# Cross-attention reciprocals spread over the partitions by a DRAM store and a repeating load, and the engines' orders written anew

## What is computed

```python
x = _layernorm(x + _L0_attn_ref(x, ...))      # theta = .5 + .2*sigmoid(qk) + .15*tanh(qk) + .1*relu(qk); softmax
x = _layernorm(x + _L0_xattn_ref(x, ctx, ctx, ...))   # softmax(q k / 4) v in chunks of 64, 16 heads
x = _layernorm(x + _L0_ffn_ref(x, ...))       # 4 of 32 experts per token, and a shared expert
```

## Time and profile before

| what | us |
|---|---|
| median of 3 runs (lowest to highest) | 883.02 (879.79 to 887.2) |
| the profiled execution | 873.37 |
| its span, first to last instruction | 871.2 |
| PE busy in the span | 801.1 (92%) |
| DVE busy | 546.1 (63%) |
| ACT busy | 461.5 (53%) |
| POOL busy | 408.3 (47%) |

### The profile page before, as it was taken

How to read it: one execution, slowest core, us unless ns; L and a number is a source line. 1 busy time by engine, 2 the same in 40 slices (tenths; PEclk the granted TensorE clock), 3 DMA queues, 4 the chain that set the end, 5 groups by cost and what they waited for, 6 DMA issues and landing times.

```text
span 871.2 us, 23658 instructions
## 1 busy us (share of the span) xinstructions
PE 801.1 (92%) x7881; PEld 658.8 (76%) x7881; DVE 546.1 (63%) x2115; ACT 461.5 (53%) x1150; POOL 408.3 (47%) x501
## 2 busy tenths in 40 slices
PE   7778999999999999999999555899999999999885
PEld 6567788888888888888887444688888888887332
DVE  2244577887788787887788852355555555554366
ACT  1455566655665666655665111466666666665133
POOL 0200235464455546464545662455656555556123
PEclk9999999999999999999999875999999999999999
DMA  6472223243324322342331124855555555552996
GB/s 222 125 174 79 80 69 103 100 136 93 121 76 142 106 103 82 133 124 94 104 127 58 67 86 134 301 163 166 165 162 159 169 165 158 161 170 91 327 401 242
DMA packets 69654, 125.06 MB, mean 144 GB/s; under 512 B 9665, under 2 KB 43329, under 8 KB 69282
## 3 DMA queue, kind: packets, MB, share of 16 engines
q1 hardware_dynamic: 51394, 81.60, 30.3%
q0 software_dynamic: 13776, 37.77, 12.1%
q10 hardware_dynamic: 4368, 4.20, 1.4%
HBM read 73.16 MB, written 50.36 MB: 142 GB/s over the span
## 4 chain that ended last, share of the span: by engine, by line
PE 78%; DMA 6%; POOL 5%; issue 4%; SPq 4%; ACT 2%; DVE 1%; ACTq 0%; POOLq 0%; DVEq 0%
PE banks L584 15%; PE banks L274 11%; PE banks L597 7%; PE banks L393 4%; SPq L623 4%; PE banks L381 3%; PE banks L354 3%; PE banks L314 3%; PE banks L335 3%; PE banks L371 3%; PE banks L326 3%; PE banks L487 3%; PE banks L518 3%; PE banks L541 3%; PE banks L529 3%
## 5 line engine op out<-in xcount | busy, mean ns | idle before, releaser
L1431 POOL DMA_INDIRECT y<-yb_tile,idcol_tile x159 | 153.0, 962 | 123.6 <-ACT yb_tile L948 121.3
L584 PE MATMUL banks<-w_expert_tile,xbT_tile 128*128 x636 | 166.4, 385 | 3.9 <-ACT xbT_tile L786 3.9
L584 PEld LDWEIGHTS banks<-w_expert_tile,xbT_tile 128*128 128x128 f32 x636 | 109.9, 193 | 13.5 <-issue 4.9
L1259 DVE COPY hbT_tile<-banks 128x128 f32<-128x128 f32 x159 | 46.4, 292 | 117.2 <-PE banks L274 117.2
L1398 POOL DMA_INDIRECT routed<-row_tile,idx_tile x64 | 63.3, 989 | 85.0 <-PE banks L410 66.5
L948 ACT ACTIVATE yb_tile<-banks,rowsb_tile 128x256 f32<-128x256 f32 x159 | 75.4, 474 | 48.8 <-PE banks L597 41.5
L597 PE MATMUL banks<-w_expert_tile,hbT_tile 128*128 x318 | 95.7, 383 | 0.0
L1366 POOL TENSOR_TENSOR rs_tile<-ve_tile,half_neg_tile 128x2 f32<-128x2 f32 x16 | 11.5, 717 | 140.6 <-DVE ve_tile L1046 140.6
L1405 POOL DMA_INDIRECT routed<-row_tile,idx_tile x64 | 65.7, 1027 | 17.7 <-issue 17.7
L942 ACT ACTIVATE gb_tile<-banks 128x128 f32<-128x128 f32 x159 | 44.2, 278 | 55.5 <-PE banks L584 55.5
L786 ACT ACTIVATE xbT_tile<-banks 128x256 f32<-128x256 f32 x159 | 59.9, 377 | 25.5 <-PE banks L274 25.2
(11 more groups left out here) (205 smaller groups left out, 1847.0 us busy)
## 6 DMA issues: line engine op xcount, KB each, us to landing
rowsb_tile<-routed SPq DMA_DIRECT2D x159, 129.0 KB, 2.2
w_expert_tile<-y SPq DMA_DIRECT2D x15, 1024.0 KB, 16.6
w_expert_tile<-w_expert SPq DMA_DIRECT2D x16, 768.0 KB, 6.3
cT_tile<-ctxT SPq DMA_DIRECT2D x16, 384.0 KB, 3.4
routed<-zrow_tile SPq DMA_DIRECT2D x1, 4128.0 KB, 22.7
xT_tile<-xT SPq DMA_DIRECT2D x16, 256.0 KB, 3.2
x_sb_tile<-x SPq DMA_DIRECT2D x16, 256.0 KB, 3.5
base<-acc_sb_tile SPq DMA_DIRECT2D x16, 256.0 KB, 3.8
```

What stands on the lines that cost most here:

```text
L584: m = e.matmul(bank[2 + u % 2][:, 0:2 * EI], xbT[u % 2][:, k * P:(k + 1) * P], w_flat[:, bass.ds(w + k * D, D)], start=k == 0, stop=k == D ...
L1259: e.tensor_copy(hbT[u % 2][:, :], bank[4 + u % 2][:, 0:EI]).then_inc(SEM["v_hbT"], 1)
L1431: e.indirect_dma_start(y, bass.IndirectOffsetOnAxis(ap=idcol[n % ROWS][:, :], axis=0), yb[n % YS][:, :], None).then_inc(SEM[f"st_y{n % YS} ...
```

## The change

- `pe_spread`, its constant and `act_num` go. `rden` (128x64) is stored to the DRAM buffer `rdd` and loaded back by two DMAs into `rsp`, each row repeated over 16 partitions. `o` reads av2's result from PSUM and `rsp` from SBUF.
- `row` and `idx` exist twice (`kM`, `vM`, `mxa` too). `pool_row` becomes `act_row`: one ACT instruction that writes all four copies.
- The PSUM banks and the order of each engine are new. Cross-attention's second half is one turn later (`scores2(t - 2)`, `x2T(t - 4)`, `shared_out(t - 5)`), so there are 22 turns.
- For space, `t12`, `prT`, `x1T` and one `kM` lie in the last 3072 columns of the expert weights (`LATE = 2` shares); those two shares are loaded in turns 17 and 18.

```diff
+        def store_den(e, i):
+            e.wait_ge(SEM["v_rden"], i + 1)
+            after(e, SEM["ld_den"], 16 * DK * i)
+            e.dma_start(rdd[i % 2].rearrange("r c q -> c r q"), rden[i % 2][:, :]).then_inc(SEM["st_den"], 16)
+        def load_den(e, i):
+            e.wait_ge(SEM["st_den"], 16 * (i + 1))
+            after(e, SEM["v_o"], i)
+            for g in range(DK):
+                e.dma_start(rsp[:, g, :], rdd[i % 2, g * 8:(g + 1) * 8].rearrange("r c (o q) -> r o (c q)", o=1)
+                            .to_broadcast([8, HD, S])).then_inc(SEM["ld_den"], 16)
...
         def vec_o(e, i, ch):
-            e.wait_ge(SEM["p_spread"], i + 1)
-            e.wait_ge(SEM["a_num"], i + 1)
-            e.tensor_tensor(f, bank[7][:, :], f, ALU.mult).then_inc(SEM["v_o"], 1)
+            e.wait_ge(SEM["p_av2"], i + 1)
+            e.wait_ge(SEM["ld_den"], 16 * DK * (i + 1))
+            e.tensor_tensor(num[:, :, :].rearrange("p a b -> p (a b)"), bank[3][:, :],
+                            rsp[:, :, :].rearrange("p a b -> p (a b)"), ALU.mult).then_inc(SEM["v_o"], 1)
...
+        def act_row(e, i):
+            e.wait_ge(SEM["a_x2"], i + 1)
+            after(e, SEM[f"st_rowa{i % 2}"], 16 * TOPK * (i // 2))
+            after(e, SEM[f"st_rowb{i % 2}"], 16 * TOPK * (i // 2))
+            e.activation(row[i % 2][:, :, :, 0:D],
+                         x2[i % 2][:, :, :].rearrange("p (k t) d -> p k t d", k=1).to_broadcast([P, TOPK, T, D]), ACT.Copy)\
+                .then_inc(SEM["a_row"], 1)
...
@@ SP
-            for t in range(nseq + 5):
+            for t in range(nseq + 6):
...
+                if live(t - 2):
+                    store_den(e, t - 2)
+                if live(t - 2):
+                    load_den(e, t - 2)
+                if 0 < t <= nseq - LATE:
                     load_rest(e, t - 1)
```

More of the change, by code:

```diff
@@ L70, in constants @@
     at, out = 0, {}
-    for name, a in zip(("ident", "before", "ones", "headmask", "denmask", "spread", "region", "upto", "blockno", "part", "nowhere"), parts):
+    for name, a in zip(("ident", "before", "ones", "headmask", "denmask", "region", "upto", "blockno", "part", "nowhere"), parts):
         out[name] = (at, a.shape[1])
@@ L158, in build @@
         den = sa("den", [P, T])
-        prT = sa("prT", [P, T, T, P])
+        prT = late(1024, 512).rearrange("p (t u q) -> p t u q", t=T, u=T)
         xc = sa("xc", [P, T, D])
@@ L167, in build @@
         x1 = sa("x1", [P, T, D])
-        x1T = sa("x1T", [P, DK, S])
+        x1T = late(2560, 512).rearrange("p (k s) -> p k s", k=DK)
         half_neg = sa("half_neg", [P, T])
         qT = sa("qT", [P, DK, S])
-        kM = sa("kM", [P, DK, S // CH, 2, CH])
-        vM = sa("vM", [P, T, NP, VW])
-        mxa = sa("mxa", [P, 4, 4])
+        kM = [sa("kM0", [P, DK, S // CH, 2, CH]),
+              late(1536, 1024).rearrange("p (k n h c) -> p k n h c", k=DK, n=S // CH, h=2)]
+        vM = [sa(f"vM{u}", [P, T, NP, VW]) for u in range(2)]
+        mxa = [sa(f"mxa{u}", [P, 4, 4]) for u in range(2)]
         mxb = [sa(f"mxb{u}", [P, 4, 4]) for u in range(2)]
@@ L189, in build @@
         acc_sb = sa("acc_sb", [P, T, D])
-        row = sa("row", [P, TOPK, T, RW])
+        rsp = sa("rsp", [P, DK, S])
+        row = [sa(f"row{u}", [P, TOPK, T, RW]) for u in range(2)]
         sc = sa("sc", [P, T, E])
@@ L208, in build @@
         slot = sa("slot", [P, T, 8])
-        idx = sa("idx", [P, T, TOPK], I32)
+        idx = [sa(f"idx{u}", [P, T, TOPK], I32) for u in range(2)]
         ctx_a.close()
@@ L1284, in _ @@
             e.memset(ev[:, :, :], -BIG)
[L1285 removed]
+            for u in range(2):
+                e.memset(vM[u][:, :, :, :], 0.0)
             ch(e.memset(macc[:, :, :], 0.0))
             e.wait_ge(SEM["g_iota"], 1)
[L1288 removed]
+            for u in range(2):
+                m = e.tensor_scalar(row[u][:, :, :, D + 1].bitcast(I32), dest_id[:, :, :], float(u * T), None, ALU.add)
+            ch(m)
             e.wait_ge(SEM["ld_const"], 16 * 5)
```

467 lines of the change are left out of this document (224 added, 243 removed).

## The result

The changed kernel takes 909.59 us (median of 4 runs, 906.94 to 919.38); the kernel before took 881.40 beside it (4 runs). The ratio is 1.033, 95% interval 1.024 to 1.043: slower, where 864.0 and a range of 855 to 880 were forecast.

The account below looks back on a forecast made before the run. PE alone was taken to set the time in mid-part. Fill 129.5, eleven turns of 27.27 and drain 69 gave 498.5 against 519.2; with 1.7 allowed, 19 less than the median 883.02: 864.0 us, range 855 to 880.

Parts of the forecast that it names:

- The step that failed: On POOL, in full turns: 2.3 us of copies go, which were off the path, so no gain or loss.
- four rivals: A and B, plus fill and drain giving nothing (872, chance 0.10) and spread's time not given back (880, chance 0.06).
- SP's queue: Next turn's xT stands behind the store, both loads and weights: 25.4 us after z against 27.27, covered by 1.9.
- A: Rival: a trip of 7.0 makes DVE's loop 27.9, some 3.5 of 19 us left, 879 us; chance 0.11.
- B: Rival: both legs at 3.8, a trip of 8.3 that sets the turn, 900 us; chance 0.09.
- the trip: Between rden and o: store, landing, two loads, landing; 5.2 us, lower bound 4.6, upper 8.3.
- DVE's rest of the loop: DVE's work besides the trip: 20.9 us, with the trip 26.1, 1.2 shorter than PE's turn.
- the spread: On PE, 1.03 us per sequence goes, so a full turn falls from 28.30 to 27.27 us if PE stays fed.
- the row copy: On ACT, one instruction of 2048 columns, about 2.1 us, with 2 us to spare before av1.
- the last stretch: From key(15) to the first row load: the same 12.5 us of scatters and landing in both kernels.
- The fill: Turns 0 to 4: xT(2) at 56, then 23, 23 and 25.5, plus 2 for the clock; turn 5 at 129.5 us.
- The drain: After the eleven full turns until key(15) is done: 21 + 21 + 25, plus 2 for the clock, 69 us.

Follow-up runs that it names:

- e1: Changed kernel with POOL's first four scatters waiting for av2 instead of scores2, so none runs beside den: 877.37 us, 0.999 of the kernel before.
- e2: Changed kernel with SP issuing the next turn's xT, x and cT loads before the store of the reciprocals: 887.63 us, 1.010 of the kernel before.
- e5: Kernel before with one group of four POOL scatters moved to wait for pTb, beside av2 and den: 916.31 us, ratio 1.038.
- e12: e3 plus four plain 129 KB stores per turn from POOL beside v and den: 882.67 us, 1.007 of the kernel before.
- e3: Changed kernel with both edits, scatters after av2 and next turn's loads before the store: 863.14 us, 0.982 of the kernel before.
- e7: e3 with the store of the reciprocals made twice, one after the other, for a longer trip: 899.94 us, 1.020 of the kernel before.
- e10: e3 plus four unused POOL additions of 128x256 per turn beside v and den: 873.41 us, 0.994 of the kernel before.
- e9: e3 with the 4128 KB zero fill cut into eight stores over turns 5 to 12: 856.24 us, 0.975 of the kernel before.

## Why the prediction was wrong

*The step that failed* is "POOL loses 2.3 us of copies, which were off the path in full turns: nothing". It asked what the edit takes off POOL, and not what the new orders put beside POOL's scatters on PE. den's 1.1 us went into the turn as a fixed price, "if PE stays fed"; in the full turns of before no scatters stand beside it, so the price held only for that neighbourhood. That it was no fixed price could be read there already: the same 32 instructions took 3.2 us in turns 1 and 2. Beside scatters den costs 2.2 us more in each turn, with a lower clock behind it in some (0.55 to 0.60 over 3.8 us). e1 (off), e2 (left on) and e5 (on in the old kernel) show it from three sides. In `after` it makes most of the difference in the eleven full turns: they took 332.1 instead of 300, of which 11 x 2.2 is 24 and the clock in four of them some 7. None of my four rivals was this one.

*Mis-sized: SP's queue.* I had xT at 25.4 after z, covered by 1.9. The loads' issue took 1.22 and not 0.9, xT's landing 6.5 and not 5.2, and den's delay came on top: rden starts at z + 18.3 instead of 16.5. Even with den at 1.1, in e1, five turns wait for xT. The forecast's sign for "A or B", a z that waits for xT, did appear in the fill, but neither A nor B held: the trip was 5.8. SP's queue made z(5) 7.8 later than forecast, and e2 takes 9.6 off there.

*Nearly right: the trip.* 5.8 us against 5.2, far from B's 8.3. The store's leg was 2.07 us, the nearest rows had 2.5 and 3.8. Two terms of mine stand on no row: the 2.0 a leg of the lower bound, beside which the store's leg was 2.07, and the 0.2 for two wake-ups, of which the first, from rden's end to the store's issue, took 0.03 (305.78 to 305.81). B's 3.8 a leg was not reached by a store alone in a full turn. With other transfers in flight the store's leg was 3.20 in e12, and 6.13 in turn 2 of e3, behind the zero fill. DVE's rest of the loop was right (20.9; e7: 20.33 + 0.55), so the cover was 0.6, and e7 and e12 show that a longer trip costs time beyond it.

*Right: the spread*, 1.03 a turn. e3's turn is 27.25 against 27.27, without any idle time on PE. *Right: the row copy*, 1.92 us on ACT, and *the last stretch*, 12.8 from key(15) to the row load.

*The fill.* xT(2) came at 55.3 (56 forecast); turns 2 to 4 took 28.4, 25.4 and 28.2 instead of 23, 23 and 25.4. z waited 2.4 us for xT at the end of turns 2 and 3, and the granted clock was low in two of the turns that such a wait stands before (0.89 in the mean of turn 2, 0.94 in turn 4), but 1.00 in turn 3; with the loads first, e2 and e3 have 1.00 in turn 4, which takes 25.97. e3 has z(5) at 127.3, close to my 129.5 but made up otherwise: z(2) at 48.4 and turn 2 of 28.7.

*The drain was too short.* From scores2(14) to the row load I had 81.8; after has 87.9 and e3, with nothing beside den in full turns, 89.8. In e3 turn 16 takes 23.6, not 21, PE waits 3.39 us for `shb` there and 6.12 for hs later. In turn 17 scatters stand beside scores2 and the transposes behind the router, and PE stops there for 0.67, 0.65 and 1.92 us with "issue". I count this as the same cost once more, which e3 didn't take away; no run tests it in that place. e3's 863.1 us are near the 864.0 on record, but by errors that cancel (the drain 8 longer, the fill 2 shorter, and executions of the kernel before some 4 us faster than those that the forecast was hung on). That is luck, and at most a number for a kernel with the scatters elsewhere.

Kept open: why indirect scatters hold these instructions and not those of 256 columns; e10 and e12 speak against POOL's additions and the plain transfer only (den 1.1 in both), and where a scatter's addresses are worked out, which e12's expectation names in brackets, no run shows. What the holes without scatters are, in turns 1 and 2 of the kernel before, is open too. And how much of e3's 1.8% over the kernel before is the spread (11 us in eleven turns) and how much the second row buffer and the fill.

## What to carry to other kernels

When an order is written anew, list for each engine what now runs beside each of its steps, not only what it waits for: a step's duration from the old trace holds for its old neighbours (den: 1.1 us in the full turns before, 3.3 after). Look at the profile for indirect DMAs of GpSimd beside dense series of short matmuls, and try to keep them apart (here one wait on the step behind them was enough: e1, row load 26.1 us sooner). Where a round trip through DRAM enters a queue, what the next turn needs is issued ahead of it (e2: row load 12.8 us sooner), and large fills are cut into pieces that fit between the others (e9: 3.9 us sooner than e3).

## What the runs showed of the hardware that I had not expected

- Four indirect scatters of 128 rows (POOL 4 x 1.27 us) beside 32 float32 matmuls of 64 columns: these took 3.2 to 3.5 us instead of 1.1 (den in after and e2, av2 in e5), mostly in holes of about 0.5 and 1.15 us. Four plain stores of the same size (e12), or four POOL additions (e10), left them at 1.1 in full turns. Where scatters and matmuls meet, no run here shows.
- Without any scatter, the same 32 matmuls took 3.2 us in turns 1 and 2 of the kernel before, with one hole of 1.9 to 2.0 us each.
- After the holes beside scatters the granted clock of after was 0.55 to 0.60 over the next 3.8 us in four turns, and 1.00 in two others with the same holes (from 305.11 and from 334.60).
- A small store that was alone took 2.07 us to the issue of the load that waits for it (after), 3.20 with four stores of 129 KB in flight (e12), and 6.13 in turn 2 of e3, with a store of 4128 KB and loads still being moved.
- An issue on SP took 11.1 to 12.6 us where a store of 4128 KB was ahead of it (12.18 in before, 11.54 in after, 11.08 in e3, 12.12 in e10, 12.63 in e12).
